# Feed-forward stage of a four-part vision network: a tile's variance moved into its own slot

## The reference

```python
t = t + attn(_ln_t(t))        # mixer: its result is added to the running t
h = relu(q_acc(q_acc(q_mul(_ln_t(t)) @ q_mul(W1).T) + q_mul(b1)))
y = q_acc(q_acc(q_mul(h) @ q_mul(W2).T) + q_mul(b2))
t = t + y
```

## Time and profile before

| | |
|---|---|
| Median of 3 runs | 4035.52 us (4033.6 to 4039.21) |
| Profiled execution, its own time | 4016.56 us |
| Its span, first to last instruction | 4014.8 us |
| PE busy | 3420.1 us (85%) |
| DVE busy, ACT busy | 1756.6 us (44%), 1812.1 us (45%) |
| Mean granted clock of TensorE | 0.942 of 2.4 GHz |

### The profile page before, as it was taken

How to read it: one execution, slowest core, us unless ns; L and a number is a source line. 1 busy time by engine, 2 the same in 40 slices (tenths; PEclk the granted TensorE clock), 3 DMA queues, 4 the chain that set the end, 5 groups by cost and what they waited for, 6 DMA issues and landing times.

```text
span 4014.8 us, 132263 instructions
## 1 busy us (share of the span) xinstructions
PE 3420.1 (85%) x59692; PEld 2370.5 (59%) x59692; DVE 1756.6 (44%) x2866; ACT 1812.1 (45%) x3411; POOL 231.9 (6%) x489
## 2 busy tenths in 40 slices
PE   3988889888898888987989879898789887898987
PEld 1737656467455584565854747547566484664855
DVE  3533455344543436434463344533445334453344
ACT  1453444533455434544345444453444534435344
POOL 3500000000000000000000000000000000000000
PEclk8989999899999999999999989999998998999999
DMA  4111000110010100101001010010100100001000
GB/s 126 40 44 28 2 14 6 41 28 3 14 29 18 28 3 14 45 2 28 3 15 44 3 27 3 15 45 3 27 2 15 44 16 14 2 16 28 22 9 14
DMA packets 24173, 88.38 MB, mean 22 GB/s; under 512 B 17843, under 2 KB 18211, under 8 KB 19643
## 3 DMA queue, kind: packets, MB, share of 16 engines
q1 hardware_dynamic: 22339, 74.72, 7.7%
q0 software_dynamic: 1280, 5.21, 0.5%
HBM read 63.86 MB, written 14.84 MB: 20 GB/s over the span
## 4 chain that ended last, share of the span: by engine, by line
PE 76%; ACT 10%; DVE 6%; issue 4%; SPq 3%; DMA 1%; ACTq 0%; DVEq 0%
PE ps L1007 76%; ACT lv L614 3%; ACT rs L619 3%; DVE area_ty L840 2%; SPq L426 1%; DVE xs L977 1%; DVE area_ty L928 1%; ACT area_ty L706 1%; ACT area_ty L700 1%; DVE area_hz L861 1%; DMA area_ty<-area_hz 1%; ACT sq L606 1%; DVE area_ty L973 0%; ACT area_ty L749 0%; DVE area_hz L877 0%
## 5 line engine op out<-in xcount | busy, mean ns | idle before, releaser
L840 DVE TENSOR_TENSOR area_ty<-ps,rs 128x448 f32<-128x448 f32 (+2 forms) x416 | 285.2, 686 | 546.9 <-ACT rs L619 546.9
L725 ACT ACTIVATE area_ty<-ps 120x448 f32<-120x448 f32 (+1 forms) x448 | 243.5, 543 | 439.7 <-PE ps L1007 439.7
L1007 PE MATMUL ps<-area_hz 32*64 32x147 f32 (+2 forms) x7180 | 371.4, 293 | 82.6 <-DVE area_hz L861 31.6
L949 DVE COPY area_ty<-ps 120x448 f32<-120x448 f32 (+1 forms) x432 | 270.0, 625 | 388.1 <-PE ps L1007 388.1
L1007 PE MATMUL ps<-area_ty,area_hz 113*64 113x49 f32 (+1 forms) x10240 | 397.0, 251 | 32.5 <-DMA area_ty<-area_hz 29.9
L1007 PE MATMUL ps<-sq,keep_sb 128*128 128x448 f32 (+1 forms) x832 | 393.6, 575 | 29.9 <-ACT sq L606 21.4
L725 ACT ACTIVATE area_hz<-ps 112x384 f32<-112x384 f32 (+2 forms) x384 | 190.9, 497 | 489.1 <-PE ps L1007 489.1
L1007 PEld LDWEIGHTS ps<-area_hz 32*64 32x64 f32 (+2 forms) x7180 | 293.3, 158 | 192.9 <-issue 165.9
L1007 PEld LDWEIGHTS ps<-area_ty,area_hz 113*64 113x64 f32 (+1 forms) x10240 | 335.0, 136 | 110.8 <-issue 110.5
L1007 PE MATMUL ps<-keep_sb,area_hz 112*56 112x56 f32 (+1 forms) x12288 | 365.7, 222 | 11.3 <-ACT area_hz L725 11.2
L1007 PEld LDWEIGHTS ps<-keep_sb,area_hz 112*56 112x56 f32 (+1 forms) x12288 | 362.1, 133 | 13.6 <-ACT area_hz L725 13.4
(11 more groups left out here) (108 smaller groups left out, 4006.4 us busy)
## 6 DMA issues: line engine op xcount, KB each, us to landing
area_hz<-f_all SPq DMA_DIRECT2D x16, 2541.0 KB
xw<-x_in SPq DMA_DIRECT2D x8, 1568.0 KB, 6.5
y_out<-xs SPq DMA_DIRECT2D x32, 294.0 KB
f_all<-piece POOLq DMA_DIRECT2D x16, 317.6 KB, 3.5
area_ty<-area_hz SPq DMA_DIRECT2D x256, 4.6 KB
area_hz<-raw_in SPq DMA_DIRECT2D x1, 2894.0 KB, 9.2
g_sb<-g_in SPq DMA_DIRECT2D x2, 1396.5 KB
g_sb<-g_in SPq DMA_DIRECT2D x1, 1470.0 KB
```

What stands on the lines that cost most here:

```text
L725: act.activation(dst, src, ACT.Relu if st in (ST_H, ST_F2) else ACT.Copy).then_inc(sc_kept, 1)
L840: ve.tensor_tensor(o, a, b, ALU.mult, **kw).then_inc(normed, 1)
L949: ins = ve.tensor_copy(dst, src)
L1007: return pe.matmul(o, a, b, start=start, stop=stop)
```

## The change

In slot `s` the variance of tile s is now taken in the same slot as its center, behind down(s-2) and up(s-1); Ln and Exp of tile s stand on ACT between the second and third half of tile s-1; the scaling of tile s stands on DVE between the second and third bias operation of tile s-1. On PE, center(s) moves ahead of down(s-2), with its wait for kept(s). In slot 0, where there are no bias operations, the scaling follows directly. No instruction is added or removed, only the order within each engine's list differs. After the change slot `s` holds:

- PE: mix(s); the next part's variance; center(s); down(s-2); up(s-1); variance(s); the next part's center.
- ACT: the next part's invert; square(s); copy of down(s-2); halves 0 and 1 of tile s-1; invert(s); half 2 of tile s-1; the next part's square.
- DVE: kept(s); the next part's scaling; bias and addition of s-2; bias operations 0 and 1 of s-1; scaling(s); bias operation 2 and the cast of s-1.

```diff
--- before.py
+++ after.py
@@ -726,13 +726,22 @@
                                            ).then_inc(sc_kept, 1)
 
             def ffn(q, l):
+                def halve(i, m):
+
+                    k = l * NT + i
+                    act.wait_ge(f_up, (q * 2 * NT + k) * HC + m + 1)
+                    if m == 0 and i >= 2:
+                        act.wait_ge(f_relu, (q * 2 * NT + k - 1) * HC)
+                    act.activation(a16[:, i % 2, m, :], ps[:, 4 + m, 0:TT], ACT.Copy
+                                   ).then_inc(f_half, 1)
+
                 for s in range(FFN_SLOTS):
-                    if 0 <= s - 1 < NT:
-                        invert(q, LN_FFN(l), s - 1)
                     if l == 0 and 0 <= s - 3 < NT:
                         invert(q, LN_MIX(1), s - 3)
                     if l == 1 and 0 <= s - 1 < NW:
                         invert(q, LN_WIN1, s - 1)
+                    if s < NT:
+                        square(q, LN_FFN(l), s)
                     if 0 <= s - 2 < NT:
                         k = l * NT + s - 2
                         act.wait_ge(f_down, q * 2 * NT + k + 1)
@@ -741,15 +750,12 @@
                         act.activation(o16[:, s % 2, :], ps[:, 7, 0:TT], ACT.Copy
                                        ).then_inc(f_out, 1)
                     if 0 <= s - 1 < NT:
-                        k = l * NT + s - 1
-                        for m in range(HC):
-                            act.wait_ge(f_up, (q * 2 * NT + k) * HC + m + 1)
-                            if m == 0 and s - 1 >= 2:
-                                act.wait_ge(f_relu, (q * 2 * NT + k - 1) * HC)
-                            act.activation(a16[:, (s - 1) % 2, m, :], ps[:, 4 + m, 0:TT], ACT.Copy
-                                           ).then_inc(f_half, 1)
+                        halve(s - 1, 0)
+                        halve(s - 1, 1)
                     if s < NT:
-                        square(q, LN_FFN(l), s)
+                        invert(q, LN_FFN(l), s)
+                    if 0 <= s - 1 < NT:
+                        halve(s - 1, 2)
                     if l == 0 and 0 <= s - 2 < NT:
                         square(q, LN_MIX(1), s - 2)
                     if l == 1 and s < NW:
@@ -959,8 +965,6 @@
                         sl = slice(TT * s, TT * s + TT)
                         ve.scalar_tensor_tensor(xs[:, sl], ps[:, 7, 0:TT], bn_bias[:, l:l + 1],
                                                 xs[:, sl], ALU.add, ALU.add).then_inc(ve_kept, 1)
-                    if 0 <= s - 1 < NT:
-                        scale(q, LN_FFN(l), s - 1, xq8[:, TT * (s - 1):TT * s], saturate=False)
                     if l == 0 and 0 <= s - 3 < NT:
                         scale_mix(q, 1, s - 3)
                     if l == 1 and 0 <= s - 1 < NW:
@@ -983,11 +987,15 @@
                                 ve.wait_ge(f_hid, q * 2 * NT + k)
                             ve.tensor_scalar(r16[:, m, :], a16[:, b, m, :], fb[:, o + m:o + m + 1],
                                              0.0, ALU.add, ALU.max).then_inc(f_relu, 1)
+                            if m == HC - 2 and s < NT:
+                                scale(q, LN_FFN(l), s, xq8[:, TT * s:TT * s + TT], saturate=False)
                         ve.wait_ge(f_relu, (q * 2 * NT + k + 1) * HC)
                         if k >= 2:
                             ve.wait_ge(f_down, q * 2 * NT + k - 1)
                         ve.sem_inc(passed_ve, 1)
                         ve.tensor_copy(hq8[:, b, :, :], r16, saturate=False).then_inc(f_hid, 1)
+                    elif s == 0:
+                        scale(q, LN_FFN(l), 0, xq8[:, 0:TT], saturate=False)
 
             for i in range(NW):
                 scale_windows(0, LN_FIRST, i)
@@ -1364,19 +1372,17 @@
                                 ins = mm(ps[o:o + RW, 7, 0:TT], mix2[:, l, RW * g:RW * g + RW],
                                          yy[a][0:YR, TT * s:TT * s + TT])
                         ins.then_inc(filled, 1)
-                    if 0 <= s - 1 < NT:
-                        variance(q, LN_FFN(l), s - 1)
                     if l == 0 and 0 <= s - 3 < NT:
                         variance(q, LN_MIX(1), s - 3)
                     if l == 1 and 0 <= s - 1 < NW:
                         variance(q, LN_WIN1, s - 1)
+                    if s < NT:
+                        pe.wait_ge(ve_kept, q * VE_FILLS + vector_fills(step_of(l, ST_FFN, s) + 1))
+                        center(q, LN_FFN(l), s, xs)
                     if 0 <= s - 2 < NT:
                         i = s - 2
                         k = q * 2 * NT + l * NT + i
-                        if s < NT:
-
-                            pe.wait_ge(ve_kept, q * VE_FILLS + vector_fills(step_of(l, ST_FFN, s) + 1))
-                        else:
+                        if s >= NT:
                             pe.wait_ge(f_out, k)
                         pe.wait_ge(f_hid, k + 1)
                         pe.sem_inc(passed_pe, 1)
@@ -1395,8 +1401,7 @@
                             mm(ps[:, 4 + m, 0:TT], ffn1[:, l, m, :], xq8[:, TT * i:TT * i + TT]
                                ).then_inc(f_up, 1)
                     if s < NT:
-                        pe.wait_ge(ve_kept, q * VE_FILLS + vector_fills(step_of(l, ST_FFN, s) + 1))
-                        center(q, LN_FFN(l), s, xs)
+                        variance(q, LN_FFN(l), s)
                     if l == 0 and 0 <= s - 2 < NT:
                         pe.wait_ge(ffn_added, q * 2 * NT + s - 1)
                         center(q, LN_MIX(1), s - 2, xs)
```

## The result

| | before | changed |
|---|---|---|
| Median (range, runs) | 4034.56 us (4021.08 to 4039.21, 4) | 4086.18 us (4079.85 to 4091.01, 4) |
| Ratio, with its 95% interval | | 1.0133 [1.0105, 1.016] |
| Profiled execution | 4016.56 us | 4091.01 us |

What follows compares the result with a forecast made beforehand. Loops of waits through several engines bound each slot (7.04 us layer 0, 6.14 layer 1). Per quad 3.99 + 5.10 - 0.4 - 1.2 = 7.5 us, +60 over 8 quads, +4 for the clock: about 4100 us, range 4078 to 4130.

Steps and rivals of the forecast that it cites:

- The loop inside one slot: In full slots of both layers, from kept(s) through PE, ACT and DVE to kept(s+1): 6.91 us (6.75 to 7.35).
- variance to Ln: Step of the full slot's loop from the variance on PE to Ln on ACT: 1.06 us.
- bias operation 2 to the cast: Step of the full slot's loop on DVE, between bias operation 2 and the cast: 0.44 us.
- ACT free for Ln: In a full slot ACT ends halves 0 and 1 near 3.7 us, against 3.79 for the variance; if late, up to 0.15.
- Openings: Slot 0 takes 5.34 us, slot 1 6.56; kept(0) to kept(6) 39.54: +5.10 in layer 1, +3.99 in layer 0.
- Ends: Kept(6) to the last addition, per stage: layer 1 -0.4 us (-1 to +0.5), layer 0 -1.2 (0 to -2).
- The clock in layer 0's opening: PE idles about 3 us before the first full slot; a clock fall costs 1.5 us, a third charged: +4 us.
- The sum: Over both layers' feed-forward stages 7.5 us per quad, +60 us in 8 quads; with the clock's +4, +64 us.
- B: Faster: the loop through scaling doesn't close, full slots fall to about PE's 5.6 us; about 4011 us; chance 0.05.
- C: No change: same loop but with shorter hand-overs, full slots near 6.0 us; 4035 us; chance 0.04.
- A: The clock falls inside layer 1's full slots, +2.6 us per slot hit, +42 us: about 4140 us; chance 0.07.
- one of the signs that the prediction named for being wrong: In layer 1, a granted clock below 1.00 would show the prediction wrong.

Runs made afterwards that it cites:

- experiment 4: Changed kernel with scaling(s) behind the cast on DVE and half 2 of s-1 ahead of Ln and Exp(s) on ACT: 4034.65 us, ratio 0.9987 to before.
- experiment 5: Changed kernel with only half 2 of s-1 moved ahead of Ln and Exp(s) on ACT, scaling left in place: 4132.72 us, ratio 1.0244 to before.
- experiment 3: Changed kernel with two, three and one unread extra PE products behind mix(1), mix(2), mix(3) in layer 0: 4085.27 us, ratio 1.0115 to before.
- experiment 2: Kernel before with the changed order in layer 0 alone, layer 1 as before: 4065.48 us, ratio 1.0063 to before.
- experiment 8: Kernel before with layer 0 in the changed order, scaling behind the cast and half 2 ahead of Ln; layer 1 as before: 4026.52 us, ratio 0.9974.
- experiment 9: As experiment 8, plus two, two and one unread PE products behind mix(1), mix(2), mix(3) in layer 0: 4018.95 us, ratio 0.9955 to before.
- experiment 1: Kernel before with the changed order in layer 1 alone, layer 0 as before: 4069.14 us, ratio 1.0074 to before.
- experiment 6: Kernel before with the next part's center and variance both around down(s-2), its ACT and DVE work reordered to match: 4057.82 us, ratio 1.0065.
- experiment 7: The changed kernel run once more with no edit, against the kernel before: 4096.05 us, ratio 1.0146.

## Why the prediction was right

It forecast 4100 us and +64 us over the median; measured were 4086.18 us, +52 us, and by the ratios of the two measurements about +54 and +59 us. The mechanism held, one term was too small, and part of how near the total came is luck, as the points below say.

- **The loop inside one slot.** Shown. The full slot is 6.85 us in both layers, worked out as 6.91. Of its terms variance to Ln was 0.95 and not 1.06, since its weight load could start ahead of it, which it couldn't in the row that the prediction used, and bias operation 2 to the cast 0.50 and not 0.44. Experiments 4 and 5 show which links it has: one more copy ahead of Ln brings 7.27, and taking bias operation and cast out from behind the scaling then brings 6.15.
- **ACT free for Ln.** Right by a hair, and the margin of 0.1 us was none: ACT's copies and PE's variance are through at the same time, and the chain of waits takes the copies. The range held it; the reading in experiment 5 that some room was left did not.
- **Openings.** 5.34 and 6.56 worked out, 5.34 and 6.61 measured in layer 1; kept(0) to kept(6) 39.54 worked out, 39.36 measured.
- **Ends.** -0.4 in layer 1 against -0.7 in the stage shown (13.05 for 13.73) and -0.5 on average; -1.2 in layer 0 against -1.3 on average.
- **The clock in layer 0's opening.** This term was mis-sized. I charged 0.5 us per stage. With slots of 5.35, 6.6 and 6.85 kept(0) to kept(6) would take 39.4 us; the profiled execution had 43.1, so some 3.8 us per stage were the clock, where before had about 1.8 (37.3 against 35.55). That is +2 us per stage, 16 us in all instead of 4. Experiment 3 shows for slots 1 and 2 that it is the clock; in slot 0 (7.03 us against 5.35 where the stage starts at the lower clock) it is read from the windows.
- **The sum.** By stages: layer 0 +35.9 and layer 1 +38.7 us in the profiled pair, 74.6 in all, with the rest of the span alike; worked out were 26 and 38. The medians give only 52 to 59. Part of this is that the profile of before was a low one: layer 1 with the same order took 388.5 to 389.9 us in experiments 2, 8 and 9, not 383.9, and layer 0 with the same order 432.7 us in experiment 1, not 429.6. Against these the changed kernel's two profiles are 61 to 67 us longer in these stages. Layer 0's part moved between those two by 8 us. The remaining few us are within the spread of the stages outside: their sum lies between 3194.7 and 3220.2 us over all kernels here but that of experiment 6. Where that spread arises is open. That +64 lies as near to the medians as it does is therefore in part luck: the clock's term was some 12 us too small and the loop 0.06 us per slot (4 us in all) too long, and with both put right the sum would be 72 us, near the 74.6 of the profiled pair and further from the medians.
- **Rivals.** B and C fall with 6.85 us in every full slot. A held in one slot of the changed kernel's profile, and in six with 0.42 us more per slot. So one of the signs that the prediction named for being wrong, a granted clock below 1.00 in layer 1, did show, in that slot and in slot 0 of two stages of experiment 7, and cost a few us; as the main cause A is out. The rule by which the prediction called A likelier is one for longer gaps than a slot has (see experiment 5).

## What to carry to other kernels

Where engines take their lists in order, sum the loops and not the work: follow the new order from one instruction back to the same instruction a slot later, through each engine's queue, and take the longest such loop, in each stage by itself. An operation with a late input, set in the middle of an engine's list, makes everything behind it late; set last, it holds up less (7.27 against 6.15 us here, experiments 5 and 4, with the same instructions). And look for the second-longest loop before you break the longest: experiment 6 ended on it. A loop that is shorter in full slots can still lose in the opening ones (slot 0 of 5.34 us instead of 3.37 in layer 1), and only the sum over the stage decides.

## What the runs showed of the hardware that was not expected

- A variance releases Ln 1.06 us after its start where its weight load starts with it, behind a wait for the square (slot 0 of the changed kernel, the slot of the earlier trace rows), and within 0.95 us where the weight load started 0.19 us ahead of it.
- The granted clock fell in a full slot of layer 1 in six of eight stages where PE's longest idle stretch in a slot was 1.33 us (0.80 in that slot, 8.54 us instead of 7.28), though PE was busy 5.38 of 7.28 us in the slot before; where it was 0.90 us, in one of 32 stages.
- Products that nobody reads held the clock where they stood (0.78 and 0.79 became 1.00), but it was low in later places instead: at the end of the same stage in five and in all eight of the stages (one and two of eight without them), and in experiment 3 at the start of layer 1 in five of eight. The median fell by about 8 us in one case, with overlapping intervals, and by nothing that can be told apart in the other.
